# Finding each edge's source row by a search over the sorted keys instead of a table of positions, in a four-layer graph kernel

## The reference

```python
edge_index = jnp.stack([src, dst])
x = _layernorm(x + gat_conv(gat_conv(x, src+loops, dst+loops, W1, ...), src+loops, dst+loops, W2, ...))
x = _layernorm(x + attention(x, Wq, bq, Wk, bk, Wv, bv, src, dst))   # softmax over the edges of a destination
x = _layernorm(x + gated_mlp(x[src], edge_attr_64, dst))             # segment_sum(sigmoid(.) * (relu(.) @ W2 + b2))
x = _layernorm(x + diffusion(x, src, dst))                           # silu(x W_in), 6 steps of segment_sum(term[src]) / deg, W_out

def gat_conv(x, src, dst, W, a_src, a_dst, b, n):   # 8 heads of 32 in the first, one of 256 in the second
    h = einsum('nd,dhf->nhf', x, W)
    logits = leaky_relu(sum(h * a_src)[src] + sum(h * a_dst)[dst], 0.2)
    e = exp(logits - segment_max(logits, dst)[dst])
    alpha = e / (segment_sum(e, dst)[dst] + 1e-16)
    return segment_sum(h[src] * alpha, dst).reshape(n, -1) + b
```

## Time and profile before

| | us |
|---|---|
| median of 3 executions (lowest, highest) | 4131.34 (4128.31, 4131.36) |
| the profiled execution | 4160.81 |
| its span | 4159.1 |

### The profile page before, as it was taken

The page is one execution under the profiler, slowest core; times in us unless marked ns, Lnnn a source line. Parts: engine busy times, 40 slices in busy tenths (PEclk is TensorE's granted clock), DMA queues, the critical chain, the costliest instruction groups (busy, mean ns, idle before and its releaser), DMA issues. The chain is left out here.

```text
span 4159.1 us, 57942 instructions
## 1 busy us (share of the span) xinstructions
PE 3324.5 (80%) x14668; PEld 2594.7 (62%) x14668; DVE 2815.1 (68%) x7889; ACT 1860.4 (45%) x5076; POOL 2545.2 (61%) x2930
## 2 busy tenths in 40 slices
PE   4999924568677699856999995499999999999775
PEld 3888712357455455433777774387878787878654
DVE  4666645559778455586666663488888888888732
ACT  2777700047523222223333331266656666666554
POOL 4777665188567566523333331487878787878667
PEclk8999955679899899955999997699999999999998
DMA  4877707724267322256333334976767676767664
GB/s 111 236 236 237 232 9 222 243 79 129 84 194 206 91 78 77 61 155 191 90 113 109 115 115 131 298 235 202 234 197 235 201 234 198 235 201 235 186 197 156
DMA packets 709256, 705.57 MB, mean 170 GB/s; under 512 B 92630, under 2 KB 663049, under 8 KB 708702
## 3 DMA queue, kind: packets, MB, share of 16 engines
q1 hardware_dynamic: 604546, 478.91, 37.5%
q0 software_dynamic: 74752, 181.57, 15.5%
q10 hardware_dynamic: 29660, 41.70, 3.0%
HBM read 422.60 MB, written 296.47 MB: 173 GB/s over the span
## 5 line engine op out<-in xcount | busy, mean ns | idle before, releaser
L620 POOL DMA_INDIRECT s_i_messages<-h,table_row x600 | 647.0, 1078 | 191.5 <-issue 129.7
L2558 PE MATMUL s_i_bank<-s_i_messages,s_i_equal 128*128 128x256 f32 x1200 | 364.5, 387 | 81.4 <-DMA s_i_messages<-h,table_row 76.8
L801 PE MATMUL s_n_bank<-w,n_xt 128*128 128x256 f32 x1280 | 308.0, 384 | 20.5 <-DMA n_xt<-in_x_t 20.5
L2595 DVE SCALAR_TENSOR_TENSOR s_i_y<-s_i_bank,s_i_scale,s_i_acc 128x256 f32<-128x256 f32 x600 | 284.6, 475 | 44.6 <-PE s_i_bank L2558 23.5
L819 PE MATMUL s_n_bank<-w_out,n_ht 128*128 128x256 f32 x1280 | 307.8, 384 | 0.9 <-ACT n_ht L829 0.9
L810 PE MATMUL s_n_bank<-n_x3t,w_in 128*128 128x256 f32 x1280 | 305.0, 381 | 0.0
L2558 PEld LDWEIGHTS s_i_bank<-s_i_messages,s_i_equal 128*128 128x128 f32 x1200 | 218.8, 193 | 112.7 <-issue 82.5
L841 ACT ACTIVATE n_w<-n_w,n_small 128x256 f32<-128x256 f32 x320 | 145.5, 502 | 313.0 <-POOL n_small L868 277.8
L801 PEld LDWEIGHTS s_n_bank<-w,n_xt 128*128 128x128 f32 x1280 | 247.2, 193 | 55.9 <-DMA n_xt<-in_x_t 20.9
L819 PEld LDWEIGHTS s_n_bank<-w_out,n_ht 128*128 128x128 f32 x1280 | 246.1, 193 | 35.6 <-ACT n_ht L829 1.3
L810 PEld LDWEIGHTS s_n_bank<-n_x3t,w_in 128*128 128x128 f32 x1280 | 244.6, 191 | 33.8 <-ACT n_x3t L699 0.2
(11 more groups left out here) (422 smaller groups left out, 9436.1 us busy)
## 6 DMA issues: line engine op xcount, KB each, us to landing
h<-s_i_y SPq DMA_DIRECT2D x600, 128.0 KB
n_xt<-in_x_t SPq DMA_DIRECT2D x160, 256.0 KB
out<-n_w SPq DMA_DIRECT2D x160, 256.0 KB
s_i_equal<-eq_tab SPq DMA_DIRECT2D x600, 64.0 KB
x<-s_x_rows SPq DMA_DIRECT2D x100, 256.0 KB
out<-s_a_hs SPq DMA_DIRECT2D x100, 128.0 KB
proj_dst<-s_a_hd SPq DMA_DIRECT2D x100, 128.0 KB
h<-s_h_rows SPq DMA_DIRECT2D x50, 256.0 KB
```

The source lines that it names most:

```text
L620: return net.nc.gpsimd.indirect_dma_start(out, None, table, bass.IndirectOffsetOnAxis(index, 0))
L801: mm = self.nc.tensor.matmul(self.pr[:, g * self.D:(g + 1) * self.D], self.XT[u][:, c, g * P:(g + 1) * P], self.net.w12[:, c, :], start=c ...
L2558: nc.tensor.matmul(banks[r % 4][:, 0:D], EQ[q % NM][:], M[q % NM][:], start=True, stop=True).then_inc(summed, 1)
L2595: V.scalar_tensor_tensor(Y[q % NY][:], banks[r % 4][:, 0:D], scale[:, s, t:t + 1], acc[:, t, :], ALU.mult, ALU.add).then_inc(added, 1)
```

## The change

The table `rep`, its puts and gets are gone. A new class `Search` finds for each source id s the row among the sorted keys: the keys are 100 rows (tiles) of 128, so the sorted list gives the first key of each tile, and a product with a staircase of the differences of keys between tiles turns "tile t has begun at s" (0 or 1 for 100 tiles) into the 128 keys of the tile in which s must lie. Of these the ones below s + 0.5 and s + 1.5 are counted with the sign function and an accumulator; if the counts differ, s is there, and its row follows.

```diff
-        self.index = sb("index", [P, T, 4], I32)
+        self.index = sb("index", [P, T, 2], I32)
+        self.end_node = sb("end_node", [P, T], I32)
...
-        keys = [(key_int[:], a["key_rows"]), (key_in_i[:], a["key_in_cols"]), (net.index[:, :, 0:2], a["index_cols"])]
+        keys = [(key_int[:], a["key_rows"]), (key_in_i[:], a["key_in_cols"]), (net.index[:], a["index_cols"])]
...
-            gp.dma_start(net.rep.rearrange("(p a) o -> p (a o)", p=125), fill[:]).then_inc(clear, 16)
-            gp.wait_ge(clear, 16)
-            gp.wait_ge(nodes_ready, 1)
-            for t in range(net.REPS[0]):
-                put_rep(net, t).then_inc(reps_out, 16)
-            gp.wait_ge(reps_out, 16 * net.REPS[0])
...
-                for t in range(first + turn_of(i), first + turn_of(i + 1)):
-                    put_rep(net, t).then_inc(reps_out, 16)
...
-            @block.gpsimd
-            def _(gp):
-                for t in range(net.REPS[1], T):
-                    put_rep(net, t).then_inc(reps_out, 16)
-                gp.wait_ge(reps_out, 16 * (T - net.REPS[1]))
-                for t in range(net.ROWS[0]):
-                    get_rep(net, t).then_inc(reps_in, 16)
-                gp.wait_ge(reps_in, 16 * net.ROWS[0])
+            @block.sync
+            def _(sp):
+                sp.dma_start(net.src_nodes[:], net.a["src_rows"].broadcast_to([T, net.R])).then_inc(nodes_in, 16)
+                sp.wait_ge(nodes_in, 16)
...
+    def reach(self, dve, g):
+        if g < self.groups:
+            Unmet.past(dve, self.spread, g - self.NB + 1)
+            W = self.TILES * P
+            self.nc.vector.tensor_scalar(self.ones[g % self.NB][:], self.net.src_nodes[:, g * W:(g + 1) * W], self.key[:, 1:2], None,
+                                         ALU.is_ge).then_inc(self.reached, 1)
...
+    def spread_keys(self, pe, g):
...
+            for k in range(self.TILES):
+                mm = self.nc.tensor.matmul(bank[:, k * P:(k + 1) * P], ones[:, k * P:(k + 1) * P], self.steps[:], start=True, stop=True)
+            mm.then_inc(self.spread, 1)
...
+    def count(self, act, g):
...
+            self.nc.scalar.activation(self.tiles_to[:, g * W:(g + 1) * W], bank[:, ::P], ACT.Copy)
+            for k in range(W):
+                t = g * W + k
+                for i in range(2):
+                    ct = self.nc.scalar.activation(self.junk[g % self.NB][:, 2 * k + i, 0:P - 1], bank[:, k * P + 1:(k + 1) * P], ACT.Sign, bias=self.node[:, 1 + i, t:t + 1],
+                                                   scale=-1.0, accum_out=self.signs[:, i, t:t + 1])
+            ct.then_inc(self.counted, 1)
...
             for k in range(N):
+                if k % 2:
+                    find.count(act, k // 2)
                 act.wait_ge(o_ready, k + 1)
...
-            for t in range(*net.ROWS):
-                get_rep(net, t).then_inc(reps_in, 16)
+            find.clear(gp)
...
                     mm.then_inc(summed, 1)
+                    if k % 2:
+                        find.spread_keys(pe, k // 2)
...
             weigh(0)
+            find.begin(dve)
...
+            find.reach(dve, 0)
             for i in range(1, N):
                 weigh(i)
+                if i % 2 == 0:
+                    find.reach(dve, i // 2)
                 join(i - 1)
             join(N - 1)
-            dve.wait_ge(reps_in, 16 * (net.ROWS[1] - net.ROWS[0]))
-            table_rows(net, Chain(dve, rows_chain), slice(0, net.ROWS[1]), is_dst, behind)
+            find.end(dve)
...
-                if i < late:
-                    get_rep(net, net.ROWS[1] + i).then_inc(reps_in, 16)
...
-        S = st.sb("d_small", [P, 32], n=2)
+        S = st.sb("d_small", [P, 32], n=4)
...
-                    past(dve, x1_ready, k - 1)
+                    past(dve, x1_ready, k - 3)
...
-    U, TURNS = 4, T // 4
+    NX, AHEAD = 6, 4
...
-                    nc.gpsimd.tensor_copy(I[u][:, 0:1], col(net.table_row, j * U + u)).then_inc(idx[u], 1)
-                    nc.gpsimd.tensor_copy(I[u][:, 1:2], col(net.dst_row, j * U + u)).then_inc(idx[u], 1)
...
+            for t in range(T):
+                past(gp, tp_made, t - NX + 1)
+                gather(net, X[t % NX][:, 0, :], net.x1, net.table_row[:, t:t + 1]).then_inc(got[t % NX], 16)
+                gather(net, X[t % NX][:, 1, :], net.x1, net.dst_row[:, t:t + 1]).then_inc(got[t % NX], 16)
...
-                nc.scalar.activation(KV[b][:], kps[b][:, 0:D], ACT.Copy).then_inc(kv[u], 1)
...
+            for i in range(T + 2):
+                biased(i)
+                score(i - 2)
+                product(i - 1)
```

More of the change, by code:

```diff
@@ L91 @@
 class Net:
-    REPS = (16, 41)
-    ROWS = (7, 60)
     def __init__(self, nc, a, ctx, edge_ctx):
@@ L1424, in load @@
                     sp.dma_start(X[k % NB][:, :, 1, :], net.proj_dst[k * G:(k + 1) * G, :, :].rearrange("g p d -> p g d")).then_inc(x_in[k % NB], 16)
-            for k in range(N):
+            for k in range(2):
+                load(k)
+            find.load(sp)
+            for k in range(2, N):
                 load(k)
@@ L1570, in gap @@
                 i = next(n) - 4
-                if late and i == late:
-                    dve.wait_ge(reps_in, 16 * late)
-                    table_rows(net, Chain(dve, rows_chain), slice(net.ROWS[1], T), is_dst, behind)
                 if i in at:
@@ new lines, in project @@
+            def project(t):
+                if 0 <= t < T:
+                    b = t % 2
+                    pe.wait_ge(xt_ready, t + 1)
+                    past(pe, q_ready, t - 1)
+                    past(pe, v_ready, t - 1)
+                    for c in range(C):
+                        mm = nc.tensor.matmul(qvs[b][:, :], XT[b][:, c, :], net.w_qv[:, c, :], start=c == 0, stop=c == C - 1)
+                    mm.then_inc(queried, 1)
+                    past(pe, k_ready, t - 1)
+                    for c in range(C):
+                        mm = nc.tensor.matmul(kps[b][:, 0:D], XT[b][:, 2 + c, :], net.w_k[:, c, :], start=c == 0, stop=c == C - 1)
+                    mm.then_inc(keyed, 1)
@@ L1867, in _ @@
+            for i in range(T + 1):
+                transposes(i)
+                project(i - 1)
         @block.scalar
         def _(act):
[L1869 to L1879 removed]
@@ L1881, in turn @@
-            def turn(j, more):
-                for u in range(U):
-                    if more or u + 1 < U:
-                        move(*following(U, j, u))
-                    keys_values(j, u)
-            turns_ahead(act, TURNS, lambda j: move(j, 0), turn)
+            for t in range(T):
+                act.wait_ge(tp_made, t + 1)
+                past(act, keyed, t - 1)
+                nc.scalar.activation(XT[t % 2][:].rearrange("p k e -> p (k e)"), tps[t % 2][:, :], ACT.Copy).then_inc(xt_ready, 1)
@@ new lines, in score, with product @@
+            def score(t):
+                if 0 <= t < T:
+                    b = t % 2
+                    dve.wait_ge(qk_ready, t + 1)
+                    V.tensor_reduce(net.scores[:, 0:H, t], heads(QK[b][:], H), AXX, ALU.add).then_inc(scored, 1)
+            def product(t):
+                if 0 <= t < T:
+                    b = t % 2
+                    dve.wait_ge(q_ready, t + 1)
+                    dve.wait_ge(k_ready, t + 1)
+                    past(dve, scored, t - 1)
+                    V.tensor_tensor(QK[b][:], Q[b][:], K[b][:], ALU.mult).then_inc(qk_ready, 1)
@@ L2746, in build @@
                 project1(net)
-                softmax(net, 1)
-                gat1(net)
+                with nc.sbuf_tensor("src_nodes", [net.T, net.R], I32) as net.src_nodes:
+                    softmax(net, 1)
+                    gat1(net)
             with nc.sbuf_tensor("scores_2", [P, 2, net.T], F32) as net.scores, nc.sbuf_tensor("out1_src", [P, net.T, net.D], F32) as net.out1_src:
```

215 lines of the change are left out of this document (105 added, 110 removed).

## The result

The changed kernel takes 3977.86 us in the median of 4 executions (3973.64 to 3978.42), the kernel before 4129.83 (4127.78 to 4131.36, 4 executions). The ratio is 0.963, 95% interval 0.9613 to 0.9647: 152 us faster, where 132 were forecast (3999 us, range 3955 to 4038). The profiled execution took 3978.4 us, so here it is no outlier.

A forecast was written before the change was run, and what follows sets the result against it. Stages run serially with different owners: POOL's issuing in several, transfers in gat1, PE nearly in project1. Terms −15 −6 −32 +6 −38 −8 −39 sum to −132 us from the median 4131.3, giving 3999 us, range 3955 to 4038.

The forecast's parts named there:

- setup, −15: Setup: index load without 8-byte runs lands earlier, and the exit without puts is shorter; −15 us (−8 to −16).
- project1, −6: Project1: 25 puts leave POOL, each delaying a power that ACT waits for; −6 us (nothing to −13).
- softmax 1, −32: Softmax 1: POOL's puts and gets go, ACT's last work ends the stage, source-id load hidden; −32 us (−10 to −33).
- gat1, +6: Gat1: search's serial parts before the loop and in the last group add +6 us; pace stays the DMA's.
- rival B: Gat1: the gets cause the slow stretch and it goes with them, 22 us less, 3977 us; chance 0.2.
- gather_out1, −38: Gather_out1: POOL's issuing sets the turns; without 40 gets, ten turns shorten; −38 us (−30 to −46).
- gat2, −8: Gat2: DVE's statistics may run three k ahead, gaining 0.2 of a 0.6 us wait; −8 us (0 to −12).
- project_qkv, −39: Project_qkv: without index copies POOL falls under PE's 3.02 us period, from 3.44; −39 us (−30 to −42).
- rival A: Whole kernel: the sum as it stands, 3999 us, own range 3985 to 4015; chance 0.48.
- C: Gat1: the search bounds the loop, ACT needing 5.6 us a pair, +22 us; 4021 to 4030 us; chance 0.2.
- D: Gather_out1 and project_qkv: removed POOL instructions were not the bound, half of −77 is lost; 4038 us; chance 0.08.
- E: Gat1: ACT's count costs more than the rest saves, slower than before; 4155 us at 1.1 us each; chance 0.04.

The follow-up runs named there:

- index_runs: Changed kernel with the index table four numbers wide again, loaded in runs of 8 bytes: 4005.29 us, setup 56.3 us instead of 43.3.
- puts_project: Changed kernel with 25 scatters of one number per slot put back on POOL in project1: 4014.75 us, the stage 493.8 us.
- before_again: The kernel before, unedited, profiled a second time: 4118.6 us, gat1 157.8 us.
- no_search: Changed kernel without the search in gat1, so later stages read wrong rows, but as many: 3969.64 us, gat1 152.7 us.
- gets_gat1: Changed kernel with 53 gathers of one number per slot put back on POOL in gat1, results unused: 3989.57 us, gat1 167.5 us.
- s_two: Changed kernel with two small buffers instead of four in gat2 and the statistics' wait one k back: 4007.24 us, the stage 257.6 us.
- gets_gather: Changed kernel with 40 gathers of one number per slot put back on POOL in gather_out1: 4013.46 us, the stage 307.9 us.

## Why the prediction was right, and where it was off

**setup, −15: −16 to −17.5.** The step held as written. The runs are 13.0 us of it, by index_runs; the exit gives the rest.

**project1, −6: −4 by the second profiles**, −14 by the first. The direction is shown by puts_project. The mechanism (a put delays the power that ACT waits for) is not: there the time went into ACT's waits for stores, and the size isn't settled.

**softmax 1, −32: −36 to −37.** The step held (end of ACT plus 0.7 us). Of the 4 us that were missed, 0.8 are the rounding of −32.8 and 0.4 the exit (0.7, not 1.1). The other 3 come from the execution that was read. Its DVE chain began 10.7 us after the stage's start (541.8 and 531.1), in before_again 8.3, in the two profiles of the changed kernel 7.0 and 8.3; and ACT's last instruction ended 68.4 us after the start, against 65.6 in before_again and 64.8 and 65.4 in the changed kernel. POOL's puts and gets, which ended the stage, ended it at 102 us in both profiles, so a late chain of ACT made the difference look smaller. The puts beside the chain are not the cause: before_again has them too.

**gat1, +6: 0 to +1.** Here two terms were wrong and one right. The search costs 5.2 us (6.5 by the second profile), where 6 were summed, and its serial parts are where the prediction saw them: 3.7 in front (2.5 forecast), 1.2 at the end (3.6). Of the pace, ACT's bound of 4.3 to 4.9 us of 4.74 was too high on two counts: a Sign starts 0.34 us after the last instead of 0.42, and the issues of the stores aren't ACT's time. ACT needs 2.9 of 5.0 us. The term that was missing is the gets': the prediction priced their removal at nothing outside the slow stretch, and it is worth 5 us, some 4 of them at the exit (before_again against no_search). Put back beside the search they cost 8 to 10; why more than in the kernel before wasn't found.

**The slow stretch and rival B.** The prediction left it out of the sum, since only the profiled execution might have had it. That was so: that execution is 29.5 us above the median, and the stretch, 20 us in gat1 by the two profiles, and project1's 10 account for these. The cause that rival B names is refuted by before_again and gets_gat1. That its number, 3977, is the measured one is luck: it is met by other terms. The prediction's estimate of 4.5 us of each DMA engine for the gets does not agree with the trace as closely as it says. It counts 6784 packets; the earlier trace rows have 1824 in the whole stage, in 0.8% of its 178 us, which is 1.4 us of each engine and some 12 ns a packet. The trace bears out the time of a packet and not their number.

**gather_out1, −38: −40 to −42**, and +40.3 when the gets come back. The step (POOL's time to issue the DMAs of a turn sets its length) held. The turn that was read, 861.08 to 872.65, has seven DMAs and not six: four gets and three gathers. A get was worth 1.0 us in the stage, less than the 1.25 from one issue to the next, since without gets POOL waits for others now and then.

**gat2, −8: −9**, and +8 in s_two. That only 0.2 of the 0.6 us wait of a k would be gained held: the period went from 4.41 to 4.21 us.

**project_qkv, −39: −37.** The bound passed from POOL to PE at 3.02 us a tile as read from the first turns. POOL's 3.44 to 3.48 was read where it is slow: over the whole stage a tile took it 3.40 us in the first profile and 3.38 in before_again, 3.33 and 3.32 in the median.

**The sum.** −132 against −148.5 between the second profiles. The 16.5 us between them are 4 in softmax 1, 4.6 in gat1, 4 in gather_out1, 2.6 in setup, 1.5 in gat2, and 4.2 in stages that the change leaves alone, less 2 each in project1 and project_qkv, where the forecast was too high. The measured 3977.9 lies within the whole range, but 7 us below the 3985 to 4015 that the prediction gave its own rival A: most terms were right in kind and a little too cautious. Rivals C, D and E fell: the pace of gat1 is unchanged (2.50 to 2.53 us a k, 2.52 in before_again), the turns of gather_out1 and the tiles of project_qkv have the lengths of rival A, and even with every Sign twice it costs only 23 us, far from the 138 that E needs.

## What to carry to other kernels

Where a stage's rows show an engine that issues without a gap, as POOL in gather_out1, an instruction removed is worth nearly its time to issue (1.0 of 1.25 us); where it waits a little in each turn, the engine behind it sets what is left, and its period can be read from a stretch in which the first was ahead. An outlier within a profile (one stretch of slow turns) should be looked for in a second profile before it is a term of a sum, and so should the end of a chain from which a difference is taken. Before work is moved into a loop that is bound by transfers, count the buffers: with four, instructions of 2 to 3 us took back most of what moving them saved; with six the whole gained 10 us.

## What the runs showed of the hardware that was not expected

**Where a stage ends with an indirect DMA, its exit grows with the indirect DMAs that POOL has issued in it.** (An indirect DMA gathers or scatters rows by a list of indices.) From the end of the last scatter, put or get to the next stage: 2.5 to 2.9 us after 2 DMAs (gat1 without gets), 6.8 after 55 (before_again, gets_gat1), 7.6 after 66 (softmax 1, before), 10.8 after 103 (gat2, changed):

```profile
1254.65 0.99 POOL L1737 DMA_INDIRECT x<-s_d_y,first_row  x1 [2.15 <-DMA x<-s_d_y,bound_row]
1266.40 0.35 SPq L1884 DMA_DIRECT2D s_e_bias<-in_bq  x1
```

That is 0.074 to 0.078 us for each. That the number is the cause is shown for gat1, where gets_gat1 changes it alone; the others are different stages. The prediction took the difference between exits (6.8 and 1.1 us) as a matter of whether POOL's puts are the last work and not of how many there were, so it had no term for gat1, where a scatter stays the last work. It is no rule for all stages. In project_qkv, with 200 such DMAs, the next stage begins 0.8 to 0.9 us after DVE's last instruction, where POOL's last gather ended 11.5 to 24 us before; in project1 it begins 2.8 us after the last store is issued, with 200 and with 225. Gather_out1's exit, from ACT's last instruction, was 6.0 us with 140 (before, and gets_gather) and 8.1 with 100. Why wasn't found.

**A stall of some 9 us in straight code, on one chip.** In project_qkv of index_runs ACT and POOL have nothing to wait for that their row shows, and PE waits for ACT:

```profile
1310.94 1.09 ACT L1925 ACTIVATE s_e_xt<-s_e_ps_t 128x512 f32<-128x512 f32 x2 [12.04 <-DMA s_d_x<-in_x,index]
...
1311.59 3.78 PE L1910 MATMUL s_e_ps_qv<-w_qv,s_e_xt 128*128 128x512 f32 x4 [7.29 <-ACT s_e_xt L1925]
```

The DMA that is named belongs to the stage before. It stood in all three profiles of straight code on that chip, in the first 27 us of the stage, in none of the others. Its cause is open. The nearest candidate is a late load of the program itself, which has a queue of its own in the profile ("instruction"). In each of the three stalls that queue has an 8 KB packet, 1.6 to 2.9 us before ACT goes on: at 1308.01 in index_runs, 1312.39 in s_two, 1327.11 in puts_project. The changed kernel has one as well, at 1284.75, 18 us after the stage's start where these come after 24 to 25, and no engine stops there. No run tests it.
